# A fused transformer block on one core: probabilities split into fp16 pairs in one step of 1024 columns, every second unit

## The reference

```
x = x + 0.5 * ffn(layernorm(x))     # gate, top 4 of 8 experts, one shared expert, SwiGLU with 341 units each
x = x + attention(layernorm(x))     # 16 heads of 64, causal, 512 x 512 scores per head
x = x + 0.5 * ffn(layernorm(x))     # the same weights again

score   = einsum('bihd,bjhd->bijh', q, k) / D ** 0.5
wmat    = softmax(score * mask + 1e+30 * (mask - 1.0), axis=2)
out     = einsum('bijh,bjhd->bihd', wmat, v).reshape(b, l, H * D) @ W_out
```

## Time and profile before

| | |
|---|---|
| median of 3 runs | 685.14 us (684.83 to 685.91) |
| span of the profiled execution, first to last instruction | 683.0 us |
| what lies around the span | 2.1 us (685.14 - 683.0) |
| TensorE clock granted over the span | 0.995 of full speed |
| attention's stretch | 124 to 571 us of the span |

### The profile page before, as it was taken

One profiled execution on the slowest core, in us unless ns is written; L12 is line 12 of the kernel. 1 busy time (PEld: TensorE's weight loads), 2 busy tenths in 40 slices (PEclk: granted clock), 3 DMA queues, 4 the chain that ended last, 5 costly groups with the idle time before them and its releaser, 6 DMA issues.

```text
span 683.0 us, 20985 instructions
## 1 busy us (share of the span) xinstructions
PE 646.1 (95%) x7846; PEld 414.1 (61%) x7846; DVE 609.6 (89%) x1701; ACT 572.8 (84%) x1110; POOL 495.7 (73%) x589
## 2 busy tenths in 40 slices
PE   5798989999999998999899999999999999999997
PEld 3465755465567565666566566665666567666665
DVE  4899799999998999899889999989999888789887
ACT  6789977898999888899978999997999997565654
POOL 3244775688899687788967889895789898566555
PEclk9999999999999999999999999999999999999999
DMA  7800000278799366588844788683678797100000
GB/s 205 258 1 1 1 2 1 54 111 148 120 129 154 57 104 120 100 140 123 145 75 79 114 140 141 125 137 56 102 125 134 144 144 110 33 1 18 17 2 16
DMA packets 226489, 62.97 MB, mean 92 GB/s; under 512 B 213202, under 2 KB 225620, under 8 KB 226388
## 3 DMA queue, kind: packets, MB, share of 16 engines
q1 hardware_dynamic: 226388, 61.64, 52.4%
HBM read 7.87 MB, written 1.05 MB: 13 GB/s over the span
## 4 chain that ended last, share of the span: by engine, by line
PE 45%; DVE 23%; ACT 16%; issue 9%; POOL 5%; DMA 1%; SPq 0%; ACTq 0%; DVEq 0%; POOLq 0%
PE bank L1068 13%; PE bank L1070 12%; PE bank L1069 12%; ACT probs L1424 6%; DVE probs L1710 4%; DVE glu L1619 3%; DVE xs L1649 3%; ACT glu L1386 3%; PE bank L1238 3%; DVE glu L1624 3%; POOL paired L1035 2%; ACT gluh L1407 2%; PE bank L1201 2%; POOL glul L1031 1%; ACT paired L1432 1%
## 5 line engine op out<-in xcount | busy, mean ns | idle before, releaser
L1031 POOL TENSOR_TENSOR glul<-glu,gluh 128x512 f16<-128x512 f32 x191 | 221.3, 1161 | 98.4 <-ACT gluh L1407 97.9
L1035 POOL TENSOR_TENSOR paired<-probs,paired 128x512 f16<-128x512 f32 x160 | 185.4, 1161 | 27.4 <-ACT paired L1432 24.5
L1386 ACT ACTIVATE glu<-bank,tanh_scale 128x512 f32<-128x512 f32 x167 | 113.3, 678 | 49.1 <-PE bank L1070 48.5
L1619 DVE SCALAR_TENSOR_TENSOR glu<-glu,bank 128x512 f32<-128x512 f32 x167 | 113.7, 681 | 24.8 <-ACT glu L1386 24.4
L1424 ACT ACTIVATE probs<-probs,exp_bias 128x128 f32<-128x128 f32 (+3 forms) x256 | 131.6, 551 | 3.6 <-POOL exp_bias L1043 3.5
L1710 DVE CUSTOM_DVE_ANT_0 probs<-bank,causal,score_scale 128x128 f32<-128x128 f32 (+3 forms) x256 | 128.0, 545 | 6.2 <-POOL paired L1035 5.0
L1068 PE MATMUL bank<-w3h,gluh 128*128 128x128 f16 x708 | 127.4, 220 | 5.9 <-POOL glul L1031 4.9
L1070 PE MATMUL bank<-w3h,glul 128*128 128x128 f16 x708 | 127.2, 220 | 0.0
L1069 PE MATMUL bank<-w3l,gluh 128*128 128x128 f16 x708 | 127.2, 220 | 0.0
L1407 ACT ACTIVATE gluh<-glu 128x512 f16<-128x512 f32 x191 | 118.5, 621 | 2.0 <-DVE glu L1624 2.0
L1624 DVE SCALAR_TENSOR_TENSOR glu<-glu,bank 128x512 f32<-128x512 f32 x167 | 114.7, 687 | 5.8
(11 more groups left out here) (236 smaller groups left out, 1619.8 us busy)
## 6 DMA issues: line engine op xcount, KB each, us to landing
pT<-paired SPq DMA_TRANSPOSE x160, 3.2
attention_raw<-in_L_attn_W_qkv SPq DMA_DIRECT2D x6, 256.0 KB, 5.3
xs<-in_L_attn_inputs SPq DMA_DIRECT2D x4, 256.0 KB, 4.7
vh<-in_L_ffn_W SPq DMA_DIRECT2D x6, 128.0 KB
pT<-in_L_ffn_W SPq DMA_DIRECT2D x6, 128.0 KB
out<-xs SPq DMA_DIRECT2D x3, 256.0 KB, 2.5
raw_more<-in_L_ffn_W SPq DMA_DIRECT2D x4, 128.0 KB
attention_raw<-in_L_attn_W_out SPq DMA_DIRECT2D x2, 256.0 KB, 6.4
```

The costliest lines, as they stand in the source:

```text
L1031: pool.tensor_tensor(glul[pair][:, :], g[:, :], gluh[pair][:, :], ALU.subtract).then_inc(glu_low)
L1035: pool.tensor_tensor(paired[n % PAIRED][:, 1, :], probs[n % PROBS][:, :], paired[n % PAIRED][:, 0, :], ALU.subtract).then_inc(probs_low)
L1386: act.activation(g[:, :], psum[b1.bank][:, :], ACT.Tanh, scale=tanh_scale[:, j:j + 1]).then_inc(tanh_made)
L1619: v.scalar_tensor_tensor(g[:, :], g[:, :], 1.0, psum[b1.bank][:, :], ALU.add, ALU.mult).then_inc(drained[b1.bank])
```

## The change

Units are split in pairs. Of two neighbours, the even one is no longer split at its own place: `turn` does nothing in the steps of even units, and in the step of the odd unit it adds one `split_probs` for both and then their two `turn`s. The copy on ScalarE and the subtraction on GpSimd become one instruction each of 2 x 512 columns, from two neighbouring buffers. The semaphores `probs_high` and `probs_low` count pairs now.

There are six buffers of probabilities instead of four. The last two lie in a place where the raw weights of experts 4 and 5 were loaded at the start (`raw12_more`), so the first `soften` that writes there waits until those weights have been used. The lags, `PAIRED` = 4 and `TURNED` = 4 stay.

```diff
-PROBS = 4
+PROBS = 6
...
         def turn(n):
             m = n - TURN_LAG
-            if 0 <= m < last:
-                self.add("split_probs", n=b * last + m)
-                self.add("turn", n=b * last + m)
+            if 0 <= m < last and m % 2:
+                self.add("split_probs", n=b * last + m - 1)
+                for of in (m - 1, m):
+                    self.add("turn", n=b * last + of)
...
+        probs_more = raw_places[2][0][:, 0:2 * 2 * 512].bitcast(F32).rearrange("p (i k) -> p i k", i=2)
+        probs_pair = [probs_all[:, 0:2, :], probs_all[:, 2:4, :], probs_more]
...
-                    q.wait_ge(probs_low, n + 1)
+                    q.wait_ge(probs_low, n // 2 + 1)
                     if n >= TURNED:
                         q.wait_ge(pv_done, n - TURNED + 1)
...
-                    q.wait_ge(probs_high, n + 1)
-                    pool.tensor_tensor(paired[n % PAIRED][:, 1, :], probs[n % PROBS][:, :],
-                                       paired[n % PAIRED][:, 0, :], ALU.subtract).then_inc(probs_low)
+                    two = slice(n % PAIRED, n % PAIRED + 2)
+                    q.wait_ge(probs_high, n // 2 + 1)
+                    pool.tensor_tensor(paired_all[:, two, 1, :], probs_pair[n % PROBS // 2],
+                                       paired_all[:, two, 0, :], ALU.subtract).then_inc(probs_low)
...
-                    q.wait_ge(exps_made, n + 1)
-                    if n >= PAIRED:
-                        q.wait_ge(turned_in[(n - PAIRED) % TURNED], 16 * ((n - PAIRED) // TURNED + 1))
-                    act.activation(paired[n % PAIRED][:, 0, :], probs[n % PROBS][:, :], ACT.Copy
-                                   ).then_inc(probs_high)
+                    two = slice(n % PAIRED, n % PAIRED + 2)
+                    q.wait_ge(exps_made, n + 2)
+                    for before in range(n - PAIRED, n - PAIRED + 2):
+                        if before >= 0:
+                            q.wait_ge(turned_in[before % TURNED], 16 * (before // TURNED + 1))
+                    act.activation(paired_all[:, two, 0, :], probs_pair[n % PROBS // 2], ACT.Copy).then_inc(probs_high)
...
                     for n, u, uses in s["units"]:
                         pr = probs[n % PROBS]
                         if n >= PROBS:
-                            q.wait_ge(probs_low, n - PROBS + 1)
+                            q.wait_ge(probs_low, (n - PROBS) // 2 + 1)
```

More of the change, by code:

```diff
@@ L544, in soften @@
                 units = [(m, of, scored[m]) for m, of in units]
-                self.add("soften", gp=gp, tiles=tiles, units=units)
+                raw_left = [(self.raw_left[of], self.measured[of]) for of in (4, 5)] if any(m in (PROBS - 2, PROBS - 1) for m, *_ in units) else []
+                self.add("soften", gp=gp, tiles=tiles, units=units, raw_left=raw_left)
                 self.add("bias", gp=gp, tiles=tiles, uses=sorted(set(use for *_, uses in units for use in uses)))
@@ L764, in macaron @@
         native_back = sb("native_back", [P, 1])
-        probs = [sb(f"probs{i}", [P, 512]) for i in range(PROBS)]
+        probs_all = sb("probs", [P, PROBS - 2, 512])
         paired_all = sb("paired", [P, PAIRED, 2, 512], F16)
@@ L769, in macaron @@
         pT = [pT_all[:, i] for i in range(TURNED)]
-        native_w = [probs[k][:, 0:NATIVE * P] for k in range(2)]
+        native_w = [probs_all[:, k, 0:NATIVE * P] for k in range(2)]
         neg_max = sb("neg_max", [P, 2, NT, 2])
@@ L782, in macaron @@
                       (sb("raw12_more", [P, 2 * 1536], F16), sb("raw3_more", [P, 2 * 1024], F16))]
+        probs_more = raw_places[2][0][:, 0:2 * 2 * 512].bitcast(F32).rearrange("p (i k) -> p i k", i=2)
+        probs_pair = [probs_all[:, 0:2, :], probs_all[:, 2:4, :], probs_more]
+        probs = [probs_pair[i // 2][:, i % 2, :] for i in range(PROBS)]
         raw12 = [raw_places[i // 2][0][:, i % 2 * 1536:(i % 2 + 1) * 1536].bitcast(F32)
@@ L1700, in vector @@
                     gp, tiles = s["gp"], s["tiles"]
+                    for left, (by, count) in s["raw_left"]:
+                        q.wait_ge(filled[left.bank], left.f + 1)
+                        q.wait_ge(measured[by], count)
                     for n, u, uses in s["units"]:
```

## The result

The changed kernel takes 704.97 us (median of 4 runs, 703.48 to 707.63); the kernel before took 685.12 us beside it. The ratio is 1.0294, with a 95% interval of 1.0272 to 1.0317. The forecast was 683.1 us with a range of 677.5 to 690.5: wrong in sign, and the time lies 14 us above the range.

What follows compares the result with a forecast made beforehand. Four engines stood close to full in attention, none alone setting the pace. Gains of 6.1 us (ScalarE 3.0, GpSimd 0.6, VectorE 2.5) against 4.1 us for late transposes gave -2.0 us: 683.1 us, range 677.5 to 690.5.

Steps and rivals of the forecast that it cites:

- GpSimd's saving: One 1024-column subtraction of 2.13 us per pair saves perhaps 0.15 us, 12 us over 80 pairs; counted as 0.6 us.
- VectorE's wait: VectorE's 5.0 us of waits for probability buffers held by GpSimd should nearly all go with six buffers; counted as 2.5 us.
- What is late next: Even units' transposes, split at the odd unit's place, come late for TensorE: 9 us of deficits, costing +4.1 us.
- first replay: Sum over all 80 pairs at unchanged pace: even units' median room 0.5 us, 29 late by 22 us together.
- the two discounts: GpSimd's shorter queue cuts lateness to 13 us, a copy 0.5 us earlier to 6 us; 9 us was taken.
- "The deficits are not paid one for one": A TensorE stall puts its later products back against ScalarE, raising the next pair's margin, so lateness costs less than its sum.
- The factor 0.45: TensorE's 45% of the old chain, used to weight 9 us of late transposes down to +4.1 us.
- The copy's wait for the earlier transposes: ScalarE's copy needs both transposes of the pair before the last; over 1 us of median room, costed at nothing.
- ScalarE's saving: One 1024-column copy at 1.08 us for two at 1.32 frees 0.24 us per pair, 19 us; counted as 3.0 us.
- Rival 1: Late transposes take over, GpSimd saves nothing and TensorE's deficits are paid one for one: slower, 691 us; chance 0.28.
- sign of being wrong on the slow side: TensorE waiting over 12 us for the transposed tile, or VectorE's and ScalarE's waits for TensorE up by more than that.
- VectorE's line with two SBUF inputs: L1584, eight instructions, could each be held a microsecond longer by GpSimd's 2.13 us subtraction: 4 us at the very worst.

Runs made afterwards that it cites:

- the kernel with the bias first: The changed kernel with GpSimd adding the exponent's bias before the double subtraction instead of behind it: 709.07 us, ratio 1.0367.
- the later copy: The changed kernel, double widths, with split and transposes moved behind the feed-forward's steps and soften, ahead of the next exponentials: 736.96 us, ratio 1.0761.

## Why the prediction was wrong

**Right.** The durations (1.055 and 2.136 us against 1.05 and 2.13), GpSimd's saving (12.8 us of a forecast 10 to 15), ScalarE's nearly (11.5 us, just under the 12 to 19 of the forecast; the 19 of the sum was too much), VectorE's wait (gone, and worth 1.9 of the 2.5 us that the sum had for it). The path from the copy to the end of the subtraction came out within 0.02 us. For the subtraction the prediction had a second estimate, 2.27 us, worked out with the 4497 ns at 2048 columns of the GPSIMD Engine Reference of the Trainium skill (3.1), at 2.17 ns a column; the trace differs, (2136 - 1161) / 512 = 1.90 ns, and the measurement decides.

**The step that failed is "What is late next".** It took 9 us of deficits at 0.45, +4.1 us. Measured were 24.7 us of waits on TensorE's weight loads and 15.4 us more idle time. Its first replay, 29 late by 22 us, is close to what came (31 waits, 24.7 us), and so is its median room of 0.5 us (0.85 measured); the two discounts from 22 down to 9, for a shorter queue on GpSimd and earlier copies, do not show in the measured waits. Three things were wrong in the step.

1. *The replay moved only the split, not what depends on GpSimd.* It kept the exponentials at the times at which they had stood. But the small `exp_bias` stands behind the split in GpSimd's order, and the prediction never names it, although its row is the next one in the earlier trace rows: the 298.64 that the prediction reads as the start of a second subtraction is this add. (The 1.11 us holds even so: two subtractions take 2.28 us together in the earlier trace rows.) Behind one subtraction of 1.16 us the exponentials waited 3.5 us for it in all; behind two, or one of 2.13 us, some 15. Its order was worth 6.3 us with single widths and 11 us with a double copy. How much of the full change's loss it is alone stays open: no kernel took the bias out of the double subtraction's way without making something else late.

2. *"The deficits are not paid one for one" holds only while there is room.* With single widths nothing speaks against it: 11.8 us of waits, with ScalarE freed of 11 us, gave 685.9 us. With the pair the median room of the even unit fell from 3.8 to 0.85 us, and there, against the kernel with the bias first, the later copy paid 27.9 us for 29.5 us more of waits. The factor 0.45 was TensorE's share of the old chain, in which all transfers had 1%; a wait that the change makes brings its own path onto the chain (DMA 8%, GpSimd 10%).

3. *The copy's wait for the earlier transposes was "at nothing", on a median of over 1 us.* It is 5.4 us in 9 places, and the chain from 316.81 us shows it linking two late pairs. The landing of the transposes is uneven (3.2 us in the median, 4.94 and 5.68 in that chain), and a pair is as late as the later of two.

**ScalarE's saving was put down to the wrong cause.** The sum counts 0.24 us a pair for one instruction in place of two. Of that, the 0.12 us of a second wait for exponentials is saved by the place, and single copies there save both such waits; the double copy keeps one and saves only the other 0.12 us, of fixed cost. At the same places the width is worth nothing on ScalarE (561.1 and 560.9 us busy). And not every copy stood behind exponentials: 136 of 160 before, 68 of 80 pairs after, which is one reason why 19 us was too much.

**The gains are not borne out at their weights.** ScalarE's 16% of the chain was to give 3.0 us. Freed of 9 us with single widths at a later place it gave nothing over six buffers, beside 7 us of waits for transposes. GpSimd's 0.6 us no run shows by itself. No run frees ScalarE and leaves the transposes as early as before, so what its freed time is worth by itself stays open.

**Rival 1** was the right one, with its point of decision: it takes over when copy to landing is over 6.8 us. In the trace after, the even units' median is 6.77 us, 39 of 80 are over 6.8, and unit 60 had 7.35. The prediction's own sign of being wrong on the slow side, over 12 us of waits for the transposed tile, came too (24.7). Rival 1 was given 0.28 and priced at 691; its upper end, 22 - 3 = +19, is near the +19.9 that was measured. It had no held bias in it, so the agreement of the sum is partly luck. A sum of the parts, from six buffers at 684.1 us: both units' splits in one place +3.7 (687.75), the bias behind both +6.3 (694.1), the copy double +6.8 (700.9), the subtraction double +4.1 (705.0). The order in which the parts are added matters: with the bias between, the double copy costs 2.0 and not 6.8 us. How much of the double subtraction's part is the odd unit's transpose, which now goes out 1.3 us behind the subtraction's end, was not tested.

**A slip beside the sum.** VectorE's line with two SBUF inputs, eight times a microsecond longer, would be 8 us and not 4. It touched nothing: its longest grew from 1.27 to 1.62 us, and nobody waited for it.

## What to carry to other kernels

Merging two instructions into one of double width saves the fixed cost of one and delays the first unit by a whole step; before counting the saving, ask how much room that unit's consumer has in its worst third of cases, not in the median. Ask also what the same two instructions would cost at the merged one's place: here the two cost ScalarE no more, since the first of them did not wait for the work just ahead. Then look at every small instruction that stands behind the merged one on an in-order engine, and at who waits for it: here the place of a 0.20 us add was worth 6 to 11 us. And a share of the old chain is no discount for a wait on a path that the change makes.

## What the runs showed of the hardware

**A small add on VectorE lasts until GpSimd's instruction beside it ends.** In the kernel with the bias on VectorE, the add of 2 or 4 columns from SBUF takes from 160 to 2010 ns. Its timeline around 144 us:

```profile
144.19 2.12 POOL L1041 TENSOR_TENSOR paired<-probs,paired 128x1024 f16<-128x1024 f32 x1 [1.74 <-ACT paired L1432]
...
144.32 2.01 DVE L1725 TENSOR_TENSOR exp_bias<-neg_max,ln_scale 128x4 f32<-128x4 f32 x1
146.26 0.68 DVE L1459 SCALAR_TENSOR_TENSOR vl<-bank,vh 128x512 f16<-128x512 f32 x1
```

It starts 0.13 us behind the subtraction and ends with it. Of the 96 adds, the 33 with no GpSimd instruction running beside them took 160 to 166 ns; of the other 63, 62 end within 0.06 us of that instruction's end. The page SBUF — State Buffer of the Trainium skill (Who interferes with whom) says that a VectorE instruction with two SBUF inputs and a GpSimd instruction that reads exclude each other for the whole instruction; this trace agrees, with 96 adds of 604 ns in the mean where 160 ns is the least. Together they took 57.9 us of VectorE where 96 of the shortest would take 15 us.

**A copy right behind its own exponential makes ScalarE busier.** In the kernel before, each of the 136 copies that stand directly behind exponentials starts after these have ended (0.03 us in the median), while the other 24 start 0.10 us before the end of the instruction ahead. With `TURN_LAG = 3` the copies are directly behind another unit's exponentials, which they do not read, and start 0.10 us before their end. The 160 copies of 512 columns count 11 us less busy time that way (572.5 against 561.7 us). That is as much as was saved in the change (11.5 us), and it is had by order alone.

**A long idle stretch of TensorE was followed by a lower clock.** In the full change with the later copy, columns: window, length, busy us of PE, PEld, DVE, ACT, POOL, granted clock, DMA share, GB/s.

```profile
336.00:338.00 2.00, 0.62 (x17) 0.49 (x14) 1.97 (x8) 2.00 (x5) 1.92 (x5) 1.00 0.85 160
338.00:340.00 2.00, 0.00 (x0) 0.00 (x0) 0.72 (x3) 2.00 (x6) 2.00 (x2) 1.00 1.16 79
340.00:342.00 2.00, 1.84 (x24) 1.84 (x25) 0.00 (x0) 0.26 (x1) 1.10 (x1) 0.50 1.20 166
342.00:344.00 2.00, 2.00 (x26) 2.00 (x25) 0.00 (x0) 0.00 (x0) 0.00 (x0) 0.65 0.85 161
```

TensorE was busy 0.62 us of 4, and then the granted clock was at the lower level, 1.2 GHz, for about 3.4 us. Matmuls of 128x128 started 0.055 us apart before the gap and 0.11 us apart behind it, while VectorE had nothing to do. The mean clock of that execution is 0.983, and TensorE is busy 8.8 us more in it than in the changed kernel's. In the profiled executions before and after the change it is 0.995 in both, so the 18.8 us between their spans owe nothing to the clock. The changed kernel's other three executions had 0.992, 0.989 and 0.987 and took 704.55, 705.39 and 707.63 us, against 703.48 us at 0.995; so the clock may carry a microsecond or two of its median.
